# Relative attention: stack loads issued by GpSimd, and the second head's relative products placed among the first head's maxima

## The reference

```
idx    = clip(k - q, -64, 64) + 64            # 129 relative positions
logits = q @ k.T + einsum(q, embK[idx])
w      = softmax(logits)
out    = w @ v + einsum(w, embV[idx])
```

## Time and profile before

| | |
|---|---|
| median of three executions | 4193.02 us |
| the profiled execution | 4175.34 us |
| its span | 4173.6 us |
| PE busy | 3820.9 us (92%) |
| DVE busy | 3370.7 us (81%) |
| ACT busy | 2863.7 us (69%) |
| POOL busy | 1500.6 us (36%) |
| mean granted PE clock | 0.941 |
| hardware queue | 606.74 MB |
| software queue (POOL's issues) | 23.34 MB |

### The profile page before, as it was taken

How to read it: one execution, slowest core, us unless ns; L and a number is a source line. 1 busy time by engine, 2 the same in 40 slices (tenths; PEclk the granted TensorE clock), 3 DMA queues, 4 the chain that set the end, 5 groups by cost and what they waited for, 6 DMA issues and landing times. The chain is left out here.

```text
span 4173.6 us, 76661 instructions
## 1 busy us (share of the span) xinstructions
PE 3820.9 (92%) x26302; PEld 2100.9 (50%) x26302; DVE 3370.7 (81%) x6323; ACT 2863.7 (69%) x5771; POOL 1500.6 (36%) x1462
## 2 busy tenths in 40 slices
PE   8599999999999999996889999999999998769998
PEld 5255555555555555554533333333333333669998
DVE  7688898898989888962769999999999893657776
ACT  4067787787878777874217777777777777236666
POOL 0456666676767666652100101001010000523333
PEclk9589999999999999998969999999999999779999
DMA  8667777777777777753762434334343421789997
GB/s 296 186 140 168 169 173 168 173 174 174 172 176 173 162 168 174 172 122 119 239 147 51 76 51 71 58 64 73 54 73 53 73 44 42 175 292 323 324 325 220
DMA packets 477915, 634.98 MB, mean 152 GB/s; under 512 B 60900, under 2 KB 403668, under 8 KB 463316
## 3 DMA queue, kind: packets, MB, share of 16 engines
q1 hardware_dynamic: 458996, 606.74, 58.0%
q0 software_dynamic: 18528, 23.34, 3.0%
HBM read 412.95 MB, written 215.89 MB: 151 GB/s over the span
## 5 line engine op out<-in xcount | busy, mean ns | idle before, releaser
L1140 ACT ACTIVATE ra_p<-ra_psS 128x512 f32<-128x512 f32 x2048 | 1112.4, 602 | 330.1 <-PE ra_psS L1211 239.7
L399 DVE TENSOR_REDUCE pa_pm<-pa_psA 128x2 f32<-128x1024 f32 x1024 | 1208.4, 1219 | 148.9 <-PE pa_psA L473 148.9
L445 ACT ACTIVATE pa_p<-pa_psS 128x512 f32<-128x512 f32 x2048 | 1063.7, 603 | 280.1 <-PE pa_psS L491 276.0
L1056 DVE TENSOR_REDUCE ra_pm<-ra_psA 128x1 f32<-128x896 f32 x1024 | 1113.4, 1087 | 167.9 <-PE ra_psA L1181 108.8
L491 PE MATMUL pa_psS<-qs,zs 50*128 50x512 f32 x2048 | 800.2, 467 | 70.5 <-ACT pa_p L445 40.7
L1181 PE MATMUL ra_psA<-zs,qs 48*128 48x512 f32 x2048 | 778.4, 466 | 78.4 <-DVE ra_pm L1058 53.6
L473 PE MATMUL pa_psA<-zs,qs 48*128 48x512 f32 x2048 | 803.7, 476 | 27.0 <-SPq L318 12.1
L1211 PE MATMUL ra_psS<-qs,zs 50*128 50x512 f32 (+3 forms) x2176 | 726.8, 419 | 2.0 <-ACT ra_p L1140 1.9
L491 PEld LDWEIGHTS pa_psS<-qs,zs 50*128 50x128 f32 x2048 | 342.6, 185 | 626.0 <-ACT pa_p L445 610.3
L1244 PE MATMUL ra_psO<-ra_p,ra_vs 128*32 128x128 f32 (+2 forms) x6400 | 570.1, 463 | 0.0
L501 PE MATMUL pa_psO<-pa_p,pa_vs 128*32 128x512 f32 x4096 | 548.0, 607 | 0.0
(11 more groups left out here) (238 smaller groups left out, 4829.6 us busy)
## 6 DMA issues: line engine op xcount, KB each, us to landing
mo_w_parts<-second_weight_parts SPq DMA_DIRECT2D x39, 2048.0 KB
relative_rows<-ra_rst SPq DMA_DIRECT2D x128, 512.0 KB
ra_blk<-window_rows SPq DMA_DIRECT2D x128, 512.0 KB, 4.2
zs<-k_halves SPq DMA_DIRECT2D x192, 248.0 KB, 7.5
mo_w_raw<-ffn_W SPq DMA_DIRECT2D x39, 1024.0 KB
qs<-q_halves SPq DMA_DIRECT2D x256, 128.0 KB, 6.1
ra_dl<-relative_rows SPq DMA_DIRECT2D x128, 256.0 KB
window_rows<-ra_pc SPq DMA_DIRECT2D x128, 256.0 KB, 7.7
```

The lines of the kernel that those rows point to most:

```text
L399: dve.reduce_max(pm[:, par, 2 * a:2 * a + 2], psA[w][:, :, :], AX.X).then_inc(s_am.h, 1)
L445: act.activation(pr[:, i % NPR, :], psS[:, slot(i), :], ACT.Exp).then_inc(s_ex.h, 1)
L1056: dve.reduce_max(pm[:, q, i, 2 * left:2 * left + 1], psA[w][:, lo:lo + 2 * G - P], AX.X).then_inc(s_far.h, 1)
L1140: act.activation(dst, psS[:, slot(t, i), :], ACT.Exp if kind == "E" else ACT.Copy).then_inc(s_cp.h, 1)
```

## The change

`stack_rows` takes the engine that issues as an argument, and GpSimd issues all stack loads. Their four semaphores are made once for the whole program with no credit, and PE's first relative product waits for nothing. SP's program loses the loads; it reads R back without anything ahead of it, `load_v` moves to the end of the turn, and at the start the writes and reads of head 1's R stand ahead of `send_m` and `write_p` of head 0. The four R of head 1 move in `first` from behind M to places behind the maxima 19, 22, 25 and 28 of head 0; POOL's masking of them moves to both sides of the first `join_p`.

More of the change, by code:

```diff
@@ L619, in rel_turns, with stack_rows, rel_attention @@
     return out
-def stack_rows(sp, qd, kd, qs, zs, b, h, w, at, done):
+def stack_rows(queue, qd, kd, qs, zs, b, h, w, at, done):
     q0, k0 = qd.offset + h * DK * T + b * S, kd.offset + h * DK * T + b * S + 64
     far, two, last = S - 64, at + 2 * DK, at + PR
-    sp.dma_start(qs[at:two, w, :].bitcast(F32), bass.AP(qd.tensor, q0, [[T, DK], [0, 2], [1, S]])).then_inc(done, 16)
-    sp.dma_start(qs[two:last, w, :].bitcast(F32), bass.AP(qd.tensor, q0 + D * T, [[T, DK], [1, S]])).then_inc(done, 16)
+    queue.dma_start(qs[at:two, w, :].bitcast(F32), bass.AP(qd.tensor, q0, [[T, DK], [0, 2], [1, S]])).then_inc(done, 16)
+    queue.dma_start(qs[two:last, w, :].bitcast(F32), bass.AP(qd.tensor, q0 + D * T, [[T, DK], [1, S]])).then_inc(done, 16)
     for side in range(2):
-        sp.dma_start(zs[at:two, w, side * far:(side + 1) * far].bitcast(F32),
+        queue.dma_start(zs[at:two, w, side * far:(side + 1) * far].bitcast(F32),
                      bass.AP(kd.tensor, k0 + side * (D * T - 64), [[T, DK], [2 * D * T, 2], [1, far]])).then_inc(done, 16)
-    sp.dma_start(zs[two:last, w, 0:2 * far].bitcast(F32).rearrange("r (s c) -> r s c", s=2),
+    queue.dma_start(zs[two:last, w, 0:2 * far].bitcast(F32).rearrange("r (s c) -> r s c", s=2),
                  bass.AP(kd.tensor, k0, [[T, DK], [D * T - 64, 2], [1, far]])).then_inc(done, 16)
-def rel_attention(nc, ident, masks, qs, zs, qd, kd, vd, e_stack, evc, ev_side, dr_r, dr_p, den_d, rec_d, ot_rows):
+def rel_attention(nc, ident, masks, stack_sems, qs, zs, qd, kd, vd, e_stack, evc, ev_side, dr_r, dr_p, den_d, rec_d, ot_rows):
     body = rel_turns()
     units = [n for n, (kind, _) in enumerate(body) if kind == "A"]
-    first = [("R", c) for c in range(4)] + [("A", a) for a in range(32)] + [("M", None)]
-    first += [("R", 4 + c) for c in range(4)] + [("A", 32 + a) for a in range(REL_AHEAD)]
+    first = [("R", c) for c in range(4)]
[4 more added lines that the diff above has]
+    first += [("M", None)] + [("A", 32 + a) for a in range(REL_AHEAD)]
     PT = len(first)
@@ L762, in _ @@
         def _(sp):
[L763 to L767, removed]
             def load_v(t, laid):
@@ L854, in _ @@
                              ptr[:, 0:NT // 4 * W].rearrange("p (i r) -> p i r", r=W)).then_inc(s_zd.h, 16)
+            write_r(1, 1, 0)
+            for c in range(3):
+                write_r(1, 1, c + 1)
+                read_r(1, 1, c)
             send_m(0, 0)
+            read_r(1, 1, 3)
             s_zd.wait(sp, 16 * NG)
             write_p(0, 0, 0)
-            for c in range(4):
-                write_r(1, 1, c)
-                read_r(1, 1, c)
             read_p(0, 0, 0)
-            s_am.wait(sp, 32)
-            load_stack(2, 0, 0, s_qa)
             for it in range(HEADS // U):
@@ L912, in _ @@
                         store_o(t, n)
+                    if p == 2 and third:
+                        load_v(t + 2, 4 * (t + 2))
             for w in range(2):
-                s_qa[w].wait(sp, NLD * HEADS // 2)
+                s_qa[w].wait(sp, NLD * (HEADS // 2 - (w == 0)))
                 s_qe[w].wait(sp, NLD * HEADS // 2)
@@ L939, in lay_v, with load_stack @@
                     s_v.wait(pool, 4 * t + n + 3)
+            def load_stack(t, at, done):
+                b, h = head(t)
+                stack_rows(pool, qd, kd, qs, zs, b, h, t % 2, at, done[t % 2].h)
             def keep(dst, src, mask, done, value):
@@ L1010, in _ @@
             pool.memset(zs[96:128, :, :].bitcast(F32), 1.0).then_inc(s_one.h, 1)
+            s_one.wait(pool, 1)
+            load_stack(0, 64, s_qe)
             lay_v(0, 0, 1)
+            part_r(1, 0)
+            part_r(1, 1)
             join_p(0, 0, 0)
-            for c in range(4):
-                part_r(1, c)
+            part_r(1, 2)
+            part_r(1, 3)
             fold_p(0, 0)
             join_p(0, 0, 1)
+            s_am.wait(pool, 32)
+            load_stack(2, 0, s_qa)
             for it in range(HEADS // U):
@@ L1188, in relative @@
                 if c == 0:
-                    s_qa[p % 2].wait(pe, NLD * loads)
+                    s_qa[p % 2].wait(pe, NLD * (loads - (p % 2 == 0)))
                 for i in range(4):
@@ L2579, in program @@
         ident = sb(top, "ident", [P, P])
+        stack_sems = [[Sem(top, nc, f"s_{n}{i}", 0) for i in range(2)] for n in ("lower", "upper")]
         with ExitStack() as one:
@@ L2588, in program @@
             rel_projection(nc, A, ident, masks, qs, zs, k_sides, e_stack, evc, ev_side, q2, kl2, kr2, v_rows)
-            rel_attention(nc, ident, masks, qs, zs, q2, k_sides, v_rows, e_stack, evc, ev_side, dr_r, dr_p,
+            rel_attention(nc, ident, masks, stack_sems, qs, zs, q2, k_sides, v_rows, e_stack, evc, ev_side, dr_r, dr_p,
                           den_d[0:UN, :], rec_d[0:UN, :], ot_rows)
```

## The result

The changed kernel takes 4310.32 us (median of 4 runs, 4290.88 to 4334.45) against 4196.88 before (the three executions above and a fourth of 4200.74): ratio 1.0279, 95% interval 1.0241 to 1.0317. It is slower, where the forecast was 4171 and faster, and it lies outside the range of 4102 to 4270.

The account below looks back on a forecast made before the run. PE was taken as the bound of relative attention. Terms -82.3 + 59.5 + 1 = -21.8 on the profiled 4175.34 gave 4153.5; the timed median stands 17.7 above, so 4171 us, range 4102 to 4270.

Parts of the forecast that it names:

- The bound, and what there was to win: Relative attention, 29 turns: PE bounds a clean turn of 50.36 us; at most 82.3 us can be won back.
- What the change takes away: In the loop, POOL's wait for the first relative read and DVE's for `ra_dl` go everywhere: up to 82.3 us removed.
- Ten issues on POOL, c = 1.1: Each loop turn: c is the time between POOL's issues, 1.1 us, likely 0.95 to 1.3; ten per turn add 59.5 us.
- full relief: Rival: c up to 0.95, POOL's lateness unfelt by PE, only PE's bound remains in the loop: 4112 us, chance 0.21.
- 910.7 + 10c: Turn from 871.80: when `part_r` 2's two maskings end on POOL; at c = 1.1 921.7, late by 1.95 us for DVE.
- the other wait, 4.69 for the block of `fold_p` 3, goes as well: Turn from 871.80: POOL reaches that fold 5.5 us later, the block already written, so its 4.69 us wait vanishes.
- 908.0 + 5c: Turn from 871.80: 908.0 is `part_r` 2's beginning on POOL with both waits taken off, before issues; 5c is five issues.
- My list of signs: What the profile after should show, such as no `ra_dl` waits mid-turn; an upper stack landing too late would refute the forecast.
- The clock's price: PE in late turns: a fall to the lower clock level costs 4.76 us; half the even turns pay, 2.4 each.
- POOL late in earnest: Rival: issues cost 1.26 us each, POOL bounds each pair of turns in the loop: 4238 us, slower, chance 0.29.
- The start: Before the loop: the fold comes 13.5 us sooner, but head 2's lower load behind it gives that back; 1 us lost.
- The rule on descriptors held up by DVE: POOL's issues: DVE operations holding the shared ports block descriptor writes; not counted; if counted, c rises by some 0.06.

Follow-up runs that it names:

- e6: The changed kernel, its order untouched, but from head 2 on each of the ten stack DMAs moves an eighth of its columns: 4087 us, ratio 0.9771.
- e9: The kernel before, its order untouched, all loads on SP, with small loads (an eighth of the columns) from head 2 on: 4098 us, ratio 0.9774.
- e12: Against the kernel before: loop's loads on SP, split into single DMAs between writes and reads; changed start, head 2's lower load before the first fold: 4093 us, ratio 0.9764.
- e5: The changed kernel with the loop's lower load right behind the upper one and, from head 2 on, loads of an eighth of the columns: 4103 us, ratio 0.9810.
- e2: The changed kernel with one edit at the start: head 2's lower load is issued ahead of the first fold; loop unchanged: 4288 us, ratio 1.0245.
- e1: The changed kernel with one edit: in the loop GpSimd issues the lower load right behind the upper load, ahead of chunk 2's fold: 4360 us, ratio 1.0442.

## Why the prediction was wrong

- **The bound, and what there was to win: right.** A clean turn is 50.36 us, and 82.3 us over 29 turns are to be had: e6, e9 and e12 win them to within a microsecond.
- **What the change takes away: right in what it names.** DVE's waits for `ra_dl` went from 20 to 2 in the loop. The cause was half right: I put it on SP's 3.93 us of issuing and on the bytes; e9 leaves only the bytes.
- **Ten issues on POOL, c = 1.1: mis-sized.** Measured 0.51 us, below every row of POOL's own DMAs that I had and near SP's bound of 0.38. (L1991, which I called plain, adds what it moves into `out`; it was no neighbour of the stack loads.) The +59.5 us that I built on it is 0 (e6). By the sum as written c = 0.51 is the "full relief" of 4112 us, 198 us from the measurement. So this was not the step that failed.
- **The step that failed: the lower load's landing in the loop, and the wait of POOL ahead of it that was taken as gone.** I costed the move of that load only by what it does to POOL (`part_r` 2 and `join_p` 1, "910.7 + 10c") and at the start by its landing. For the loop no term asked when the load itself lands against PE's first relative product. And "the other wait, 4.69 for the block of `fold_p` 3, goes as well" was wrong: it stayed, with 6.02 us in the turn from 816.25 and 154.2 in all. By the working the load begins at 908.0 + 5c, at the measured c 38.7 us into the turn; e6, where the wait is gone, has 39.4. The changed kernel has 45.9. From there 2.5 us of issuing and the 8.9 of landing end at 57.3, for a product that a clean turn has at 50.8; by the same sizes it would have landed at 50.1 from 38.7, just in time (an estimate, for no run has the one without the other). So the load in flight made the read late, the read POOL, and POOL the next load: a chain that the sum has nowhere. My list of signs named the upper stack's landing, and it was the lower's. In the kernel before the load left at 894.64, 22.8 us into the turn.
- **The clock's price was too low.** I took 4.76 us per fall. In the turn from 867.29 the gaps of 5.25 us cost 14.85, so 9.6 beyond the gaps, at a granted clock of 0.82. Over the 29 turns PE is busy for 1575.37 us at a granted clock of 0.90, against 1425.10 at 1.00 in e6: 150 of the excess of 210.1 are the same instructions taking longer, and not waiting.
- **The rivals: the slower side was named with the wrong mechanism.** "POOL late in earnest" gave 4238 by c = 1.26. The only turns that the runs show late by POOL's issues alone are the two of e5, some 10 us in all.
- **The start: right in kind.** The fold came 8.6 us sooner, not 13.5 (DVE now waits 7.96 us at 133.57 for head 0's first write, with head 1's load in flight since 122.54), and head 2's load gave it back; I allowed 4.3 of loss and took 1, measured 5.3. e2 shows that the load's place alone does it.
- **The rule on descriptors held up by DVE, cited in the prediction from the Trainium skill (SBUF — State Buffer, section "SBUF: two separate sides"):** no run here shows it. POOL's issues took 0.51 us beside a DVE that was busy for most of the turn.

What stays open: the 29 us that the profiled execution lost behind the attention; the two late issues; and whether POOL's queue has a share of its own, for no run sent full loads in pieces from POOL. Late turns of 58 to 65 us often alternate with clean ones of 50.4. The late turn from 867.29 sent its load 11.6 us ahead of its end (at 920.93), and the next is clean; the one from 816.25 sent it 5.1 us ahead, and the next is late. What sets this lead from turn to turn was not looked for.

## What to carry to other kernels

When a transfer is moved to another issuer, look first at where in the turn it now leaves and when its first reader wants it; the issue's own price was nothing here. Here a load of 1.1 MB made late the small transfers that were in flight with it, so a program like this one, which depends on short round trips through DRAM, wants its loads in pieces between these trips, not in one block. Lumps were slow from either queue; the pieces were tried on SP's alone. A wait may be taken off a sum only if what it waits for is shown to come sooner. A test that keeps the order and shrinks the bytes tells the price of the issues from that of the bytes in one run.

## What the runs showed of the hardware

- POOL issued a plain DMA of 16 or 32 rows every 0.51 us, plus 0.29 us ahead of the first; two of the changed kernel's issues came 2.6 us late, for a cause that stays open. SP needed 0.58 to 0.59 at the median for the same ones, and for all five 3.0 us (from 894.64) to 3.9 (from 720.10) beside POOL's 2.5.
- One DMA of a load landed in 7.5 us (median) from SP's queue and in 7.6 from POOL's. Off SP's queue it still made a read-back on SP's queue take 12.5 us (issued at 845.42, with one load in flight, in POOL's hands at 857.90) and 20.9 when two loads were in flight (e1), but small writes there fell from 7.7 to 3.1 us.
- Two gaps on PE, 5.25 us together, at the border of a turn made it 14.85 us longer, at a granted clock of 0.82 over that turn.
